# Writing finished tokens by four indexed scatters from GpSimd instead of one plain store from SyncE

## What is computed

```python
t = x1.reshape(8192, 64)                       # after the attention half
xf = layernorm(t)
top_w, top_i = top_k(xf @ Wg + bg, 2)
w_dense = sum(one_hot(top_i, 8) * softmax(top_w)[..., None], axis=1)
for e in range(8):
    out += w_dense[:, e:e+1] * (gelu(xf @ W1[e] + b1[e]) @ W2[e] + b2[e])
return t + out
```

## Time and profile before

| | before |
|---|---|
| time, median of 3 runs | 601.84 us (601.73 to 603.74) |
| profiled execution: span | 602.3 us |
| its own time outside the profile | not recorded apart from the span |
| TensorE matmul busy | 582.0 us, 97% |
| VectorE busy | 392.7 us, 65% |
| ScalarE busy | 382.3 us, 63% |
| GpSimd busy | 177.9 us, 30% |
| stores of `ob` | 16 DMAs of 128 KB, median 2.0 us from issue to landing |

### The profile page before, as it was taken

How to read it: one execution, slowest core, us unless ns; L and a number is a source line. 1 busy time by engine, 2 the same in 40 slices (tenths; PEclk the granted TensorE clock), 3 DMA queues, 4 the chain that set the end, 5 groups by cost and what they waited for, 6 DMA issues and landing times.

```text
span 602.3 us, 12032 instructions
## 1 busy us (share of the span) xinstructions
PE 582.0 (97%) x3585; PEld 268.5 (45%) x3585; DVE 392.7 (65%) x1216; ACT 382.3 (63%) x670; POOL 177.9 (30%) x246
## 2 busy tenths in 40 slices
PE   6999899999999999999889999999999999999996
PEld 5465566666666666655532232223223223223221
DVE  5798898777777887778935654455554545554522
ACT  3556666556565565546567866676766677766673
POOL 3044344344434434342302121222121122121122
PEclk9999999999999999999999999999999999999999
DMA  8900000000000000000000000000000000000000
GB/s 230 194 11 2 2 1 1 2 0 0 0 0 0 0 0 0 0 1 1 1 2 1 9 10 9 3 9 11 9 9 7 2 9 9 9 9 9 0 10 17
DMA packets 23421, 8.98 MB, mean 15 GB/s; under 512 B 19786, under 2 KB 23328, under 8 KB 23392
## 3 DMA queue, kind: packets, MB, share of 16 engines
q1 hardware_dynamic: 22848, 8.49, 6.3%
q10 hardware_dynamic: 544, 0.13, 0.1%
HBM read 6.38 MB, written 2.10 MB: 14 GB/s over the span
## 4 chain that ended last, share of the span: by engine, by line
PE 74%; DVE 11%; issue 8%; POOL 3%; ACT 2%; DMA 0%; POOLq 0%; SPq 0%; DVEq 0%; ACTq 0%
PE bank L1181 21%; PE bank L1193 10%; PE bank L1194 9%; PE bank L1052 6%; PE bank L1152 5%; PE bank L1121 4%; PE bank L998 3%; PE bank L1142 3%; PE bank L1033 3%; PE bank L1073 2%; DVE mx L764 2%; DVE sm L772 2%; PE bank L1210 2%; POOL pn L436 1%; DVE bt L822 1%
## 5 line engine op out<-in xcount | busy, mean ns | idle before, releaser
L600 ACT ACTIVATE wloc<-bank,cols 128x512 f32<-128x512 f32 x256 | 161.7, 688 | 39.9 <-PE bank L1194 39.8
L1181 PE MATMUL bank<-wloc,w_sb 128*64 128x512 f32 x512 | 139.1, 617 | 0.3 <-ACT wloc L600 0.3
L436 POOL TENSOR_TENSOR pn<-pe_,rs 128x256 f32<-128x256 f32 x128 | 77.4, 626 | 181.9 <-DVE rs L775 171.6
L888 DVE SCALAR_TENSOR_TENSOR wloc<-bank,cols,zs 128x512 f32<-128x512 f32 x64 | 47.9, 749 | 113.6 <-PE bank L1181 113.5
L1193 PE MATMUL bank<-xs,w_hi 128*128 128x512 f16 x256 | 97.8, 382 | 0.0
L1194 PE MATMUL bank<-xs,w_lo 128*128 128x512 f16 x256 | 97.0, 379 | 0.0
L543 ACT ACTIVATE pe_<-sc 128x512 f32<-128x512 f32 x64 | 40.3, 630 | 50.2 <-DVE sc L767 50.2
L1052 PE MATMUL bank<-bd,aa 128*64 128x128 f32 x1024 | 70.9, 281 | 0.5 <-ACT aa L536 0.5
L1152 PE MATMUL bank<-pt,bt 128*128 128x256 f32 x256 | 66.0, 380 | 0.0
L456 POOL TENSOR_TENSOR acc<-acc,wloc 128x512 f32<-128x512 f32 x32 | 40.8, 1274 | 85.0 <-DVE wloc L888 85.0
L1052 PEld LDWEIGHTS bank<-bd,aa 128*64 128x64 f32 x1024 | 55.5, 138 | 23.2 <-issue 17.0
(11 more groups left out here) (152 smaller groups left out, 726.5 us busy)
## 6 DMA issues: line engine op xcount, KB each, us to landing
wloc<-in_L_conv_w_local SPq DMA_DIRECT2D x2, 1152.0 KB, 7.7
out<-ob SPq DMA_DIRECT2D x16, 128.0 KB, 2.0
x_sb<-in_x SPq DMA_DIRECT2D x3, 512.0 KB, 10.8
w_sb<-in_L_ffn_W SPq DMA_DIRECT2D x3, 512.0 KB, 7.4
x_sb<-in_x SPq DMA_DIRECT2D x2, 256.0 KB, 3.4
cv<-cv SPq DMA_DIRECT2D x1, 144.0 KB, 2.4
wo_h<-in_L_conv_w_out ACTq DMA_DIRECT2D x1, 64.0 KB, 2.1
wq_sb<-in_L_conv_w_q SPq DMA_DIRECT2D x1, 64.0 KB, 2.3
```

The source lines that it names most:

```text
L436: ins = nc.gpsimd.tensor_tensor(pn[:, v % 2, :].rearrange("p (a y k c) -> p a k y c", a=PAIRS, k=2, c=WSZ)[:, :, k], pe_[:, v % 2].rearran ...
L600: nc.scalar.activation(hh[:, c % 4], hidb[c % 4][:], ACT.Gelu, scale=1.0 / (XS * WS), bias=cols[:, 2 * e + k:2 * e + k + 1]).then_inc(gelu ...
L888: nc.vector.scalar_tensor_tensor(yw[:, p], outb[p % 2][:], cols[:, 16 + p:17 + p], wb[:, t[1] % 2, p], ALU.add, ALU.mult).then_inc(yw_read ...
L1181: last = nc.tensor.matmul(outb[(c // 4) % 2][hf:hf + C, :], w2_sb[:, e, k], hh[:, c % 4], start=(k == 0), stop=(k == 1))
```

## The change

The store moves from SyncE's stream to GpSimd's. `store(prv)` waits for `out_ready` and issues four indirect DMAs, one for each tile of 128 tokens; each writes 128 rows of 256 bytes to the rows of `out` that are listed, one a partition, in `orow`. The list is made once by an iota (`rows_ready`), and for each later group by one `tensor_scalar` that adds 512 to the other buffer's 128 x 4 numbers (`store_rows`). Both calls stand at the head of GpSimd's step, ahead of its three adds. `stored[b]` now counts four DMAs a group, so the waits of VectorE and SyncE on it have four times the value. GpSimd's loop over groups is written out in full, 17 steps in place of 8 copies of the body and a loop. SyncE is left with the wait at the end.

```diff
+        orow = sb("orow", [P, 2, TG], U32)
...
+        rows_ready = sem("rows_ready")
...
-            def body(g):
-                prv = sh(g, -1)
-                if real(prv):
-                    b = prv[1] % 2
-                    wait(sp, out_ready, at(prv, 1, 1))
-                    sp.dma_start(out_tiles[:, bass.ds(idx(prv, TG), TG), :], ob[:, b]).then_inc(stored[b], 16)
-            steps(sp, body, 0, NG)
             for b in range(2):
-                sp.wait_ge(stored[b], 16 * (NG // 2))
+                sp.wait_ge(stored[b], 16 * TG * (NG // 2))
...
+            nc.gpsimd.iota(orow[:, 0], [[P, TG]], base=0, channel_multiplier=1).then_inc(rows_ready, 1)
             nc.gpsimd.memset(xsp[:], 0.0).then_inc(zeroed, 1)
...
+            def store(t):
+                b = t[1] % 2
+                wait(pool, out_ready, at(t, 1, 1))
+                wait(pool, rows_ready, at(t, 1, 1))
+                for v in range(TG):
+                    nc.gpsimd.indirect_dma_start(out=out, out_offset=bass.IndirectOffsetOnAxis(ap=orow[:, b, v:v + 1], axis=0),
+                                                 in_=ob[:, b, v], in_offset=None).then_inc(stored[b], 16)
+            def store_rows(t):
+                b = t[1] % 2
+                wait(pool, stored[b], at(sh(t, -b), 8 * TG, 0))
+                wait(pool, rows_ready, at(t, 1, 0))
+                nc.gpsimd.tensor_scalar(orow[:, b], orow[:, 1 - b], GT, None, ALU.add).then_inc(rows_ready, 1)
             def experts(g):
+                prv = sh(g, -1)
+                if real(prv):
+                    store(prv)
                 if not real(g):
                     return
+                if real(prv):
+                    store_rows(g)
                 b = g[1] % 2
                 wait(pool, f_done, at(g, 1, -1))
...
-            steps(pool, experts, 0, NG - 1)
+            for s in range(NG + 1):
+                experts((None, s))
...
-                            wait(dve, stored[b], at(sh(prv, -b), 8, 0))
+                            wait(dve, stored[b], at(sh(prv, -b), 8 * TG, 0))
```

More of the change, by code:

```diff
@@ L301, in program @@
         x_tiles = x.rearrange("(t p) d -> p t d", p=P)
-        out_tiles = out.rearrange("(t p) d -> p t d", p=P)
         dots = [banks[0], banks[1]]
```

## The result

The changed kernel takes 612.89 us (median of 4 runs, 611.71 to 614.06); the kernel before, with a further run, 602.79. The ratio is 1.016, with a 95% interval of 1.0136 to 1.0184: 1.6% slower, where 0.8% was forecast, and just outside the range (603.5 to 612.0). Runs of every kernel here fall into two groups 2 us apart (before 601.7 and 603.7, after 611.7 and 614.0); the gap is there by the first `ob`, which starts 335.0 to 335.6 or 337.3 to 337.8 us into the span.

What follows compares the result with a forecast made beforehand. TensorE bounds the kernel (matmuls busy 582.0 of 602.3 us), but at the end the store is the path. Steps 0, last group 0 and tail +4.9 on the median 601.84 gave 606.7 us, range 603.5 to 612.

Steps and rivals of the forecast that it cites:

- the tail's sum: After the last `ob`: four scatters issued in sequence, then the landing, 6.9 us against 2.0 before, +4.9 us.
- Clearing up after the last: After the last scatter: possible work that no row shows, named as something that would make the prediction wrong; no size given.
- T: GpSimd's time for one scatter of 128 rows, put at 1.27 us, range 0.8 to 1.7; slower begins at 0.8.
- The steps: Expert steps with a store: scatters, 5.2 us with row list, lie in GpSimd's idle time; cost 0.
- The part on ports: Expert steps: VectorE and GpSimd hold each other up; scatters lose at most 4 x 0.3 us, inside the slack.
- the slack of the normalise: Expert steps: L1007 starts 1.25 us after VectorE's L680 ends, so TensorE does not wait for it.
- Rival 2: Steps: scatters hold VectorE's normalise up, 3.9 us in each of 13 steps; time 609 to 658 us; chance 0.12.
- Rivals 1: Tail: scatters are cheap, 0.37 to 0.62 us each, adding 1.3 to 2.3 us, no change told; chance 0.15.
- 3: Steps and end: GpSimd becomes the bound at 2.4 to 2.6 us a scatter; time 615 to 628 us; chance 0.04.
- 4: Steps: faster by over 0.5%, as L674's lost 1.05 us comes back in 13 steps; chance 0.02.
- The last group's third add: Last group: the add before it ends at 596.1, 0.8 us early, so it is not delayed; cost 0.
- The base: Whole kernel: profiled span 602.3 us taken as 0.5 above the runs' median 601.84, to which 4.9 was added.

Runs made afterwards that it cites:

- experiment 9: Kernel before, with the last group alone stored by four scatters at the end of GpSimd's stream, the other fifteen by SyncE; 606.29 us, ratio 1.0069.
- Experiment 3: Changed kernel, but in step 1 alone the four scatters and row list stand after GpSimd's second add; 610.91 us, ratio 1.0141.
- experiment 2: Changed kernel, but the last group stored by one plain DMA from SyncE, groups 0 to 14 by scatters; 606.09 us, ratio 1.007.
- 6: Changed kernel, but only the eight even groups stored by scatters (32 in all), the odd ones by SyncE; 604.38 us, ratio 1.0032.

## Why the prediction was wrong

**The step that failed: the tail's sum stopped at the landing.** "Nothing else runs, so the difference is on the path" was true of the span up to the last landing, and the sum had nothing behind it. 4.0 us stood there: GpSimd's drain, which takes 0.082 us for each of 64 DMAs and in the changed kernel ends 5.3 us after the last scatter's issue. "Clearing up after the last" was named as what would make the prediction wrong, with no price and no rival of its own. The trace of before had the instruction, at 1.37 us, but with no DMA in front of it, so its price by the DMA could not be read there.

**Tail up to the landing: right in kind, 0.6 us too high.** T was put at 1.27 us and a little between; the scatters come every 1.26 us, as 0.96 of work and 0.30 between. Predicted +4.9, in the changed kernel +4.3, alone +4.4 (experiment 9, the drain of four included). Most of the difference is the last landing, which came 1.2 us after the end of its issue where 1.6 was taken from SyncE's; the rest is a gap that was counted behind the last scatter too, less a slower start (0.28 us after `ob` instead of 0.1). T was right by luck in part: it was taken from GpSimd's pass over 512 elements, and is made of 0.96 us of work and a gap that no row of before could show. The Trainium skill (DMA: Bandwidth & Descriptors, "Latency and other measured facts") gives about 1 us up to the first byte for a DMA from GpSimd, and the 0.96 us of one scatter in the trace is near that. By the trace another 0.30 us lies between two scatters, 0.9 us of the tail.

**The steps: zero for 14 of 15, 1.6 us in step 1.** The scatters lie in GpSimd's idle time, the third add is on time, L1227 never waits for it before the end, and step lengths are unchanged from step 2 on, all as predicted; so is the first add, 4.6 us later against `ob`. One reading behind it was off without effect: the two idle times at L1210 that an add ended are one and the same, at the end of the kernel, the weight load's 3.06 us and the matmul's 2.18. No step before had one. The part on ports failed in one place: the slack of the normalise was read from one step in the middle (1.25 us) and taken for all. In step 1 before there were 0.3 us. The instructions that the adds hold up fell just there. Experiment 3 took the loss back by moving the scatters behind the second add.

**Rival 2 (scatters hold VectorE up): refuted, with the right mechanism on the wrong instruction.** An add still holds up the small instructions of VectorE's normalise where it falls on them. Scatters do not, or hardly: in the step shown four L691 take 0.309 to 0.502 us each beside two of them, and no L691 beside a scatter alone takes longer. The Trainium skill (SBUF — State Buffer, "Who interferes with whom") says that where a VectorE instruction needs both ports, whichever engine starts first has them for the whole instruction. The trace agrees for adds (one L691 of step 1 takes 1.39 us, with the second add) and not for scatters.

**Rivals 1, 3 and 4.** Scatters are not cheap enough (T with the gap 1.26, decision at 0.8), GpSimd is no bound, and the 1 us that VectorE regained in each step was worth nothing, as said. The last group's third add came 0.6 us after its second had ended, not the 0.8 of the sum, and was not delayed.

**The clock** was not in the prediction: 0.5 us. In the three kernels with step 1's loss the last transposes took 1.11 us (the changed one), 1.12 (experiment 2) and 0.83 (6), as the granted clock fell to 0.50 before or amid them; in all others they took 0.66 at 1.00, after the same 2.2 us of idling. So the 0.5 us goes with step 1's loss, and experiment 3 took both back. By what path is not shown: the time of the transposes does not decide it, since experiment 2 had them at 597.0 at the low clock and 3 at 597.8 at the high one.

**The base.** The prediction set the span of 602.3 against a median of 601.84. The profiled run was one of the upper group: with 1.8 us between span and time, as in most later runs, its own time would be 604.1. The differences are not touched by it.

## What to carry to other kernels

A DMA moved to GpSimd has three prices: its issue, on the path wherever nobody else is at work (here 1.26 us a scatter, at the end only); what its neighbours on GpSimd do once they are pushed back (an add holds up whatever small VectorE instruction it now falls on, so look for the step with the least slack, not a typical one); and the closing drain, by the number of DMAs. The last one can be hidden: let another engine store the last piece, or drain in the steps while GpSimd is idle. When a sum for the end of a kernel is made, it should run to the last instruction of every engine, not to the landing of the last result.

## What the runs showed of the hardware

- GpSimd's drain takes 0.082 us for each DMA of 128 rows that it has issued since its last drain, landed or not, plain or indirect, of 16 bytes a row or 256 (49 and 98 small ones: 4.1 and 8.1 us; 64 in three kernels: 5.3 us each).
- A plain DMA costs GpSimd 0.54 us with one run of 256 bytes a partition and 0.77 with four; a scatter of 128 rows costs 0.96 (the first of a group 1.06, the first of the program 1.19), and 0.30 lie between two scatters. Landing, from the start of the issue: 1.7, 2.4 and 2.1 us.
- A GpSimd add held some VectorE instructions until it ended (0.17 us became 1.19 to 1.20, and 0.30 became 1.27 to 1.39) and not others: L905, begun under an add, kept its 0.75 us. A scatter alone stretched an instruction of 0.30 us to 0.51 at most.
- What the 2 us between the two groups of runs are, before the first `ob` of every kernel, is open: no run was made for it. Nor was it tried whether a drain's work could be spread thinner than four DMAs at a time.
